# Windowed attention in a four-stage hybrid kernel: scores as 32x32 tiles of plain queries and head-masked keys, probabilities turned by VectorE, mixing by 32 keys

## The reference

```
q, k, v = heads(x @ w_qkv.T)                    # 16 heads of 8 features
scores  = q . k / sqrt(8)
allowed = (j <= i) & (i - j < 64)               # query i sees 64 keys: itself and the 63 before it
ctx     = softmax(where(allowed, scores, -inf)) @ v
out     = ctx @ w_out.T + b_out
```

## Time and profile before

| | us |
|---|---|
| runs (3): median | 1002.17 |
| runs: lowest to highest | 1000.75 to 1002.77 |
| the profiled execution: span from its first to its last instruction | 997.6 |
| PE busy in the span | 911.7 |
| ACT busy | 611.6 |
| DVE busy | 647.7 |
| POOL busy | 661.2 |

### The profile page before, as it was taken

How to read it: one execution, slowest core, us unless ns; L and a number is a source line. 1 busy time by engine, 2 the same in 40 slices (tenths; PEclk the granted TensorE clock), 3 DMA queues, 4 the chain that set the end, 5 groups by cost and what they waited for, 6 DMA issues and landing times.

```text
span 997.6 us, 16805 instructions
## 1 busy us (share of the span) xinstructions
PE 911.7 (91%) x5472; PEld 627.0 (63%) x5472; DVE 647.7 (65%) x1447; ACT 611.6 (61%) x1875; POOL 661.2 (66%) x610
## 2 busy tenths in 40 slices
PE   3267899899999999999999999999999998999998
PEld 1144566686666666586666666677666666657665
DVE  5886867688658638697739737787735347437432
ACT  4345566984664575895674575797455377386432
POOL 7676878657688649666759857756765545646554
PEclk8567999989999999999999999999999999999999
DMA  5005252014353524610433534520333560350452
GB/s 185 0 3 135 46 129 72 16 45 108 88 127 87 121 79 96 155 44 12 96 87 88 127 98 85 146 65 18 84 99 81 139 156 12 84 132 12 85 129 63
DMA packets 64762, 85.68 MB, mean 86 GB/s; under 512 B 5218, under 2 KB 30627, under 8 KB 64419
## 3 DMA queue, kind: packets, MB, share of 16 engines
q1 hardware_dynamic: 64674, 84.62, 35.2%
HBM read 79.32 MB, written 5.28 MB: 85 GB/s over the span
## 4 chain that ended last, share of the span: by engine, by line
PE 61%; ACT 11%; POOL 7%; issue 5%; DVE 4%; DVEq 0%; ACTq 0%; POOLq 0%
PE bank L1545 16%; PE bank L1522 8%; PE bank L1524 8%; PE bank L1523 8%; ACT probs L1089 5%; PE bank L1581 4%; PE bank L1566 4%; POOL work L881 3%; PE bank L1595 2%; PE bank L1559 1%; PE bank L1405 1%; POOL kv_terms L846 1%; DVE probsT L1345 1%; PE bank L1399 1%; POOL rstd L833 1%
## 5 line engine op out<-in xcount | busy, mean ns | idle before, releaser
L881 POOL TENSOR_TENSOR work<-work,spread_w 128x512 f32<-128x512 f32 x256 | 336.3, 1325 | 165.4 <-DVE work L1303 162.3
L1303 DVE TENSOR_TENSOR work<-work,bank 128x512 f32<-128x512 f32 x256 | 173.6, 681 | 214.0 <-ACT work L1064 128.1
L1545 PE MATMUL bank<-work,down_w 128*128 128x512 f32 x512 | 263.9, 599 | 9.3 <-POOL work L881 7.4
L1064 ACT ACTIVATE work<-bank 128x512 f32<-128x512 f32 x256 | 151.2, 596 | 182.1 <-PE bank L1524 178.6
L1089 ACT ACTIVATE probs<-bank,neg_max 128x96 f32<-128x96 f32 x512 | 166.0, 382 | 8.2 <-DVE neg_max L1331 5.7
L1522 PE MATMUL bank<-z_hi,gate_hi 128*128 128x512 f32 x256 | 167.0, 652 | 3.6 <-ACT elu L974 2.0
L889 POOL TENSOR_TENSOR probs<-probs,prob_inv 128x768 f32<-128x768 f32 x64 | 94.1, 1470 | 74.0 <-DVE prob_inv L1339 74.0
L1089 ACT ACTIVATION_READ_ACCUMULATOR probs<-bank,neg_max 128x1 f32 x512 | 125.6, 248 | 0.0
L1545 PEld LDWEIGHTS bank<-work,down_w 128*128 128x128 f32 x512 | 94.6, 189 | 40.5 <-POOL work L881 15.0
L1524 PE MATMUL bank<-z_hi,gate_lo 128*128 128x512 f32 x256 | 102.4, 400 | 0.0
L1522 PE MATMUL bank<-z_hi,up_hi 128*128 128x512 f32 x256 | 102.0, 398 | 0.0
(11 more groups left out here) (154 smaller groups left out, 1466.2 us busy)
## 6 DMA issues: line engine op xcount, KB each, us to landing
spread_w<-comb_dram SPq DMA_DIRECT2D x96, 512.0 KB, 6.7
spread_w<-comb_dram SPq DMA_DIRECT2D x128, 128.0 KB, 3.0
vals<-v_dram SPq DMA_DIRECT2D x16, 384.0 KB, 4.1
x_buf<-x SPq DMA_DIRECT2D x8, 256.0 KB, 3.4
v_dram<-v_tok SPq DMA_DIRECT2D x8, 256.0 KB, 4.5
out<-xs SPq DMA_DIRECT2D x8, 256.0 KB, 3.8
spread_w<-wg SPq DMA_DIRECT2D x1, 1024.0 KB, 6.5
spread_w<-wu SPq DMA_DIRECT2D x1, 1024.0 KB, 8.5
```

The source lines that it names most:

```text
L881: pool.tensor_tensor(work[:, n % WORK], work[:, n % WORK], spread_w[:, n // EACH % 2, s % EACH], ALU.mult).then_inc(hid_gated, 1)
L1064: act.activation(work[:, n % WORK], bank[GATE_BANKS[ring_of(row, f, s)]], ACT.Silu).then_inc(silu_ready, 1)
L1303: dve.tensor_tensor(work[:, n % WORK], work[:, n % WORK], bank[UP_BANKS[ring_of(row, f, s)]], ALU.mult).then_inc(gated_ready, 1)
L1545: pe.matmul(bank[Y_BANK], down_w[:, c], work[:, n % WORK], start=(c == 0), stop=(c == CH - 1)).then_inc(down_done, 1)
```

## The change

Scores. The query block is now the plain 32 queries x 32 features (`queriesT`), and the keys are the ones that are laid out four times, each copy masked to one head and scaled (`head_keys`). A score matmul has 32 rows (features of hg) and 32 columns (queries of block b) and is 384 wide (four heads x 96 keys); the mask matmul is cut in the same way, one for each block. So an output partition is the query and a column is (head, key). For each hg there are four mask matmuls and four f32 matmuls on four different column groups of the array. `keys` on ACT becomes four instructions and `queries` one plain copy.

Turning. PE's transposes, their bank waits and DVE's four copies go. DVE transposes each half of a tile's normalised probabilities in 32x32 squares, SBUF to SBUF, two instructions of 128x768.

Mixing. With 32 keys as rows and 32 features as columns, the 96 keys of a block become three accumulating matmuls, 48 in a tile. Blocks 0 and 2 go first, then, after a wait on PE's own semaphore `mix_begun`, blocks 1 and 3. The results stand in halves of the banks 5 and 6. The values are loaded three times, shifted by 32 keys, with three transfers for two tiles. In the next pass, `up` into bank 5 waits for the last tile's `mix_taken`; `gate` into bank 4 waits for nothing.

```diff
+MIX_BANK = 5
+PHASES = ((0, 2), (1, 3))
...
-        seqT, keysT = sb("seqT", [P, WIN + SEQ]), sb("keysT", [P, WIN + SEQ])
-        qm = sb("qm", [P, G, NB * T, HG, QB])
-        vals = sb("vals", [KW, 2, 2 * NB, D])
+        seqT, head_keys = sb("seqT", [P, WIN + SEQ]), sb("head_keys", [P, HG, WIN + SEQ])
+        queriesT = sb("queriesT", [P, SEQ])
+        vals = sb("vals", [P, 2, KW // QB, 2, D])
...
-        probsT = sb("probsT", [KW, NB, HG * P])
+        probsT = sb("probsT", [P, HG * HG, KW])
...
-        bank = [ctx.enter_context(nc.psum_tensor(f"bank{i}", [P, 512], F32))[:] for i in range(8)]
+        low = [ctx.enter_context(nc.psum_tensor(f"bank{i}", [P, 512], F32))[:] for i in range(MIX_BANK)]
+        mixed = ctx.enter_context(nc.psum_tensor("mixed", [P, 2, 512], F32))[:]
+        bank = low + [mixed[:, 0], mixed[:, 1],
+                      ctx.enter_context(nc.psum_tensor(f"bank{SIDE_BANK}", [P, 512], F32))[:]]
...
             def load_windows(row, pair):
                 wait(sp, mix_ready, tile(row, 2 * pair) - 2)
-                windows = bass.AP(v_dram.tensor, 2 * P * pair * D, [[D, KW], [QB * D, 2 * NB], [1, D]])
-                sp.dma_start(vals[:, pair % 2], windows).then_inc(vals_loaded[pair % 2], 16)
+                for past in range(KW // QB):
+                    shifted = bass.AP(v_dram.tensor, (2 * P * pair + QB * past) * D, [[D, P], [P * D, 2], [1, D]])
+                    sp.dma_start(vals[:, pair % 2, past], shifted).then_inc(vals_loaded[pair % 2], 16)
...
-                const(pool.memset(vals[0:WIN, 0, 0], 0.0))
-                pool.memset(keysT[:, 0:WIN], 0.0).then_inc(masks_ready, 1)
+                const(pool.memset(vals[0:WIN, 0, 0, 0], 0.0))
+                pool.memset(head_keys[:, :, 0:WIN], 0.0).then_inc(masks_ready, 1)
...
             def keys(row, g):
-                copy_side(keysT[:, WIN + GT * g:WIN + GT * (g + 1)], row, "keys", g)
-
-            def queries(row, g):
 
                 if row == 0 and g == 0:
                     act.wait_ge(head_mask_ready, 2)
-                side_product(row, "queries", g)
+                side_product(row, "keys", g)
                 for j in range(HG):
-                    a = act.activation(qm[:, g, :, j, :], side.rearrange("p (b q) -> p b q", q=QB),
+                    a = act.activation(head_keys[:, j, WIN + GT * g:WIN + GT * (g + 1)], side,
                                        ACT.Copy, scale=q_mask[:, j:j + 1])
                 a.then_inc(side_taken, 1)
+
+            def queries(row, g):
+                copy_side(queriesT[:, GT * g:GT * (g + 1)], row, "queries", g)
 
...
-                wait(act, probsT_ready, (tile(row, i) - 1) * NB)
+                wait(act, probs_turned, 2 * (tile(row, i) - 1))
...
+            step(dve.tensor_copy(head_mask2[:].rearrange("p (b j) -> p b j", j=HG),
+                                 head_mask[:].unsqueeze(1).broadcast_to([P, NB // 2, HG])))
...
-            def turned(row, i, blocks):
+            def turned(row, i, half):
                 wait(dve, mix_ready, tile(row, i))
-                for b in blocks:
-                    dve.wait_ge(probsT_ready, tile(row, i) * NB + b + 1)
-                    dve.tensor_copy(probsT[:, b], bank[4 + b % 2][0:KW, :]).then_inc(probsT_copied, 1)
+                dve.wait_ge(probs_normed, 2 * tile(row, i) + half + 1)
+                part = slice(half * HALF_BLOCKS, (half + 1) * HALF_BLOCKS)
+                dve.transpose(probsT[:, part].rearrange("p h k -> p (h k)"),
+                              probs[:, i % 2, part].rearrange("p h k -> p (h k)")).then_inc(probs_turned, 1)
...
                 wait(dve, mix_picked, tile(row, i))
-                as_heads = lambda a: a.rearrange("p (b j q) -> p b j q", b=NB, j=HG)
-                of_head = head_mask[:].unsqueeze(1).unsqueeze(3).broadcast_to([P, NB, HG, QB])
-                dve.tensor_tensor(as_heads(mix_all[:]), as_heads(bank[6]), of_head, ALU.mult).then_inc(mix_taken, 1)
+                two_banks = mixed[:, :, 0:NB // 2 * P].rearrange("p c (b j q) -> p c (b j) q", j=HG, q=QB)
+                dve.tensor_tensor(mix_all[:].rearrange("p (c m q) -> p c m q", c=2, q=QB), two_banks,
+                                  head_mask2[:].unsqueeze(1).unsqueeze(3).broadcast_to([P, 2, NB // 2 * HG, QB]),
+                                  ALU.mult).then_inc(mix_taken, 1)
...
-                    elif after is not None:
-                        for b in (NB - 2, NB - 1):
-                            pe.wait_ge(*copied_of(after[0], after[2] - 1, b))
+                    elif after is not None and banks[ring_of_chunk] == MIX_BANK:
+                        pe.wait_ge(mix_taken, tile(after[0], after[2]))
...
@@ -1555,48 +1561,45 @@
                 for hg in pair:
                     if (row, i) not in END_AT:
                         pe.wait_ge(probs_ready, (tile(row, i) - 1) * HG + hg + 1)
-                    feats = slice(QB * hg, QB * (hg + 1))
-                    pe.matmul(bank[hg][:, 0:NB * KW], same_query[feats].rearrange("p j q -> p (j q)"),
-                              window[feats, min(i, 1)].rearrange("p b k -> p (b k)"), start=True, stop=False,
-                              tile_position=(QB * hg, 0), skip_group_check=True)
                 for b in range(NB):
-                    first = P * i + QB * b
+                    of_block = slice(QB * b, QB * (b + 1))
                     for hg in pair:
                         feats = slice(QB * hg, QB * (hg + 1))
-                        mm = pe.matmul(bank[hg][:, KW * b:KW * (b + 1)],
-                                       qm[feats, i // T, NB * (i % T) + b].rearrange("p j q -> p (j q)"),
-                                       keysT[feats, first:first + KW], start=False, stop=(b == NB - 1),
-                                       tile_position=(QB * hg, 0), skip_group_check=True)
+                        pe.matmul(bank[hg][of_block, 0:HG * KW].rearrange("p (j k) -> p j k", k=KW), same_query[feats, 0],
+                                  window[feats, min(i, 1), b].unsqueeze(1).broadcast_to([QB, HG, KW]), start=True,
+                                  stop=False, tile_position=(QB * hg, QB * b), skip_group_check=True)
+                for b in range(NB):
+                    of_block, first = slice(QB * b, QB * (b + 1)), P * i + QB * b
+                    for hg in pair:
+                        feats = slice(QB * hg, QB * (hg + 1))
+                        mm = pe.matmul(bank[hg][of_block, 0:HG * KW].rearrange("p (j k) -> p j k", k=KW),
+                                       queriesT[feats, first:first + QB], head_keys[feats, :, first:first + KW],
+                                       start=False, stop=True, tile_position=(QB * hg, QB * b), skip_group_check=True)
                         if b == NB - 1:
                             mm.then_inc(scores_ready, 1)
 
-            def turn_probs(row, i, blocks):
-                pe.wait_ge(probs_normed, 2 * (tile(row, i) + 1))
-                for b in blocks:
-                    if b >= 2:
-                        pe.wait_ge(*copied_of(row, i, b - 2))
-                    elif tile(row, i):
-                        pe.wait_ge(*copied_of(0, tile(row, i) - 1, b + 2))
-                    for hg in range(HG):
-                        mm = pe.transpose(bank[4 + b % 2][0:KW, P * hg:P * (hg + 1)],
-                                          probs[:, i % 2, hg * NB + b], ident[:])
-                    mm.then_inc(probsT_ready, 1)
-
             def mix(row, i):
-                pe.wait_ge(vals_loaded[i // 2 % 2], 16 * (tile(row, i) // 4 + 1))
+                pe.wait_ge(vals_loaded[i // 2 % 2], 16 * (KW // QB) * (tile(row, i) // 4 + 1))
                 if (row, i) in END_AT:
                     pe.wait_ge(y_copied, END_AT[row, i])
                 else:
                     pe.wait_ge(mix_taken, tile(row, i))
-                for b in range(NB):
-                    pe.wait_ge(*copied_of(row, i, b))
-                    for hg in range(HG):
-                        feats = slice(QB * hg, QB * (hg + 1))
-                        mm = pe.matmul(bank[6][feats, P * b:P * (b + 1)],
-                                       vals[:, i // 2 % 2, NB * (i % 2) + b, QB * hg:QB * (hg + 1)],
-                                       probsT[:, b, P * hg:P * (hg + 1)], start=True, stop=True,
-                                       tile_position=(0, QB * hg))
-                mm.then_inc(mix_ready, 1)
+                pe.wait_ge(probs_turned, 2 * tile(row, i) + 2)
+                for phase, blocks in enumerate(PHASES):
+                    if phase:
+                        pe.wait_ge(mix_begun, tile(row, i) + 1)
+                    for past in range(KW // QB):
+                        for hg in range(HG):
+                            for b in blocks:
+                                keys_of = slice(QB * b, QB * (b + 1))
+                                mm = pe.matmul(
```

(16 more changed lines are left out.)

25 lines of the change are left out of this document (12 added, 13 removed).

## The result

The changed kernel takes 1045.35 us in the median of 4 runs (1042.01 to 1053.04); the kernel before took 1001.83 us in the same session. The ratio is 1.0457, 95% interval 1.0413 to 1.0502: slower, where 992 us was forecast, and outside the forecast's range of 984 to 1022. The profiled execution has a span of 1042.3 us, 44.7 more than the earlier trace rows, with a mean granted clock of 0.875 (before: 0.962).

The account below looks back on a forecast made before the run. PE, ACT and DVE were taken as nearly even, the chain on PE. Terms -3.5, -4, -5, -0.6, -1, +0.8 gave -13.3, with clock +3 -10.3: 997.6 to 987.3 profiled, 992 us median; range 984 to 1022.

Parts of the forecast that it names:

- Eight small matmuls at once: PE, scores and mix: row and column groups together run eight matmuls at once; score pair 1.0 us, mix 1.8 to 2.0.
- (b): Rival, PE: only four small matmuls at once, so PE needs 7.3 us a tile and bounds: 1055 us; chance 0.12.
- (c): Rival, PE's mix: 32 ns between records is PE's rate of taking them, so the tile is 5.85 us: 1012; chance 0.11.
- DVE's transposes at 0.9: DVE: each of a tile's two transposes takes 0.9 us, by the nearest f32 sum; bounds 0.46 and 1.8.
- (d): Rival, DVE: f32 transposes take two passes, 1.8 us each, so the tile is 6.1 us: 1021 us; chance 0.09.
- The loop that decides: Full swing: a loop over DVE, PE's mix and ACT takes 10.4 us for two tiles, 5.2 a tile against 5.40.
- rival (e): The change buys nothing: the loop is 0.2 us longer than summed and row 0 hangs on its norms: 1001; chance 0.05.
- rival (a): PE's clock falls in the other rows too; at a third of the time the tile is 5.8 us: 1006; chance 0.18.
- +3 for row 0: PE's clock: allowance of 3 us lost in row 0, where the clock fell already.
- Rows 1 to 3: -3.5: Attention tiles in full swing: 17 tiles gain 0.2 us each, -3.5 us.
- row 0: -4: Row 0's attention part: 13 us of PE work go, ACT idle for only 13.2; -4 us, bounds 0 and -9.
- -5: The five drains: DVE's transposes and the mix end earlier than the old copies and mix, -1 us each.

Follow-up runs that it names:

- the score part alone: Kernel before with only plain queries, head-masked keys and 32x32 score tiles; PE still turns the probabilities, one head at a time: 1016.77 us, ratio 1.0144.
- 48 small tiles: Changed kernel plus unread matmuls of 32x32 weights by 384 columns, 24 in each of two places of a tile but a part's first: 1045.32 us, ratio 1.0425.
- full-array work: Changed kernel plus eight unread matmuls of 128x128 weights by 512 columns, only in the second and third tile of each part: 1054.12 us, ratio 1.0533.
- split wait: Changed kernel; exponentials of a tile's first two groups wait only for the first transposing of the tile before last: 1040.72 us, ratio 1.0409.
- early transposings: Changed kernel with both transposings of tile i-1 moved on DVE ahead of both reciprocals of tile i: 1044.83 us, ratio 1.0427.
- four full-array matmuls a tile: Changed kernel plus four unread matmuls of 128x128 weights by 512 columns in each attention tile but a part's first: 1071.62 us, ratio 1.0701.
- both cures: Changed kernel with both transposings ahead of the reciprocals and unread 32x32 matmuls in PE's pauses: 1022.40 us with 24 a tile, 1020.37 with 32.

## Why the prediction was wrong, point by point

- **Eight small matmuls at once: right.** Score pair 1.0 us forecast and measured; mix 1.8 to 2.0 forecast, 1.94 measured. Rivals (b) and (c) are out: the 48 matmul records of a phase, on eight squares, start within 0.66 us, 14 ns apart. The Trainium skill's floor of about 25 ns ("TensorE: Matmul & The Clock Gate", section "Wait — 56ns, not 53.3ns?") isn't met by these records on different squares; the measurement decides.
- **DVE's transposes at 0.9: right** (0.93 to 0.98), so (d) is out. The copies of scaled keys take 0.69 each, 0.60 forecast.
- **The loop that decides: the step that failed.** The forecast put the second transposing of tile i-1 behind the last exponential of tile i, rightly, and then followed it only through the mix. It overlooked who else waits for it: the exponentials of tile i+1, by the wait on `probs_turned` in their own code. That loop is one tile long, 5.07 + 0.25 + 0.94 and hand-overs: 6.45 at full clock. Splitting the wait removed it where nothing else was late (5.06). The same step went wrong a second time: the loop through the mix, 5.2 forecast, measures 5.57 at full clock and 6.97 at half, because it passes both transposings, the take, the maxima and the mix in every tile, not once in two. With the forecast's own prices that is 0.9 + 0.6 + 0.94 + 0.11 + 0.9 + 2.0 = 5.45 and hand-overs, already more than the 5.40 of the kernel before. So even with the clock at 1.00 and the first loop cured, full swing had nothing to gain in this order of DVE's calls; rival (e), a loop 0.2 longer, was near in that.
- **The clock, and rival (a): the fall came, its counter-argument failed.** The clock fell in all parts, in rows 1 to 3 behind pauses of 1.23 or 1.24 and 2.42 us; a term of +3 for row 0 alone was too little. Not only the missing transposes open these pauses: with them kept, the score part alone has 1.25, 0.43 and 0.92 us there, and falls of 6.8 us. Nor is it shown that the length of a pause decides: with 48 small tiles a tile 1.24 and 1.46 us were left in row 1 and the clock held, with full-array work 1.24 and 1.31 and it fell. "A slower PE is a busier PE, which ends the pauses" is what the runs contradict: 44.3 us at 0.50 with PE busy 39.95, and 0.50 still at 8.56 of 8.70. And the 7.6 us of PE work that (a) took for a tile at half clock isn't what bounds it, but the mix, 3.2 long at that clock, in DVE's loop. Nor does it follow from 3.8 and 7.6 that half clock decides from a quarter of the time on: the mean of the two passes 5.2 when 37% of the tiles are at half clock.
- **The sum.** Rows 1 to 3: -3.5 forecast (for 17 tiles; 24 less two in each of four parts are 16, -3.2), +23.0 measured; row 0: -4, +5.9. The stretches between and behind the parts' tiles, with the drains in them, for which -5 was forecast, gave +15.5; 12.6 of it lies behind rows 0 and 1, where the clock was at 0.50 until 252.0 and from 484.2 to 497.8, and behind row 2, where the clock held, it is -0.1. PE doesn't wait in front of `up` behind a drain, as forecast. The loop and the clock don't add: the first loop is a floor of 6.45 us a tile at full clock, the second one of 6.97 at half, so curing one shows the other. That fits the runs with one cure (split wait, early transposings, 48 small tiles), which stay between 1040 and 1045.

Left open: what brings PE's clock down in these parts and back to 1.00 (with 48 small tiles a fall ended soon, with four full-array matmuls a tile it lasted 54.6 us), what holds the last 19 us with both cures, most of them outside the tiles, and what the score tiles are worth by themselves.

## What to carry to other kernels

When a step moves to another engine, list every instruction that waits for its semaphore, and for each what now stands ahead of the step in its new queue; here one forgotten reader closed a loop of ACT and DVE. When two tiles are in flight, look first for a loop that closes within one of them, on two engines. Before working out a gain from relieving an engine, look at what its work covered: where PE kept its transposes, it paused 0.43 and 0.92 us at the start of a part, and without them 2.42 at once. And when one cure changes nothing, look for a second floor at the same height before dropping the theory.

## What was not expected of the hardware

PE stayed at 0.50 for 44.3 us with 90% busy time, and was at 0.50 with 8.56 of 8.70 us busy; in the run with 48 small tiles a tile, a fall in row 1 lasted about 3.4 us (458.2 to 461.6) only. In the mix the hand-over between the phases, in which PE's weight loads wait for its own last matmul, costs 0.35 us at full clock and 0.57 at half. In each phase 48 matmuls on eight different 32x32 squares start 14 ns apart.
